# The order of TensorE's work within a slot: projections, transpositions, side work, scores and values

## The reference

```
for i in range(6):
    # 16 heads of 64; window of 32 tokens: each query sees its own and the previous 32
    q, k, v = split(shift_tokens(x) @ Wqkv[i])
    q, k = rotary(l2norm(q) * qs), rotary(l2norm(k) * ks)
    x = softmax(8 * q k^T, masked to the window) v @ Wo[i] + x
    xn = layernorm(shift_tokens(x)) * g + b
    a, gate = split(xn @ W1[i] + b1)            # 341 features each
    x = a * gelu(gate) @ W2[i] + b2 + x
out = xn0 + linear_branch * silu(x)
```

## Time and profile before

| | |
|---|---|
| median of three executions | 1900.61 us (1897.97 to 1902.92) |
| the profiled execution | 1898.34 us |
| its span, first to last instruction | 1896.5 us |
| TensorE busy | 1663.9 us, 88% |
| VectorE busy | 1436.9 us, 76% |
| ScalarE busy | 1345.7 us, 71% |
| GpSimd busy | 1298.5 us, 68% |
| mean granted TensorE clock | 0.971 |
| DMA | 66.13 MB, q1 at 11.5% of 16 engines |

### The profile page before, as it was taken

One profiled execution on the slowest core, in us unless ns is written; L12 is line 12 of the kernel. 1 busy time (PEld: TensorE's weight loads), 2 busy tenths in 40 slices (PEclk: granted clock), 3 DMA queues, 4 the chain that ended last, 5 costly groups with the idle time before them and its releaser, 6 DMA issues.

```text
span 1896.5 us, 68500 instructions
## 1 busy us (share of the span) xinstructions
PE 1663.9 (88%) x25968; PEld 1306.9 (69%) x26160; DVE 1436.9 (76%) x3041; ACT 1345.7 (71%) x2656; POOL 1298.5 (68%) x1283
## 2 busy tenths in 40 slices
PE   7789899899899899889989989988998998899873
PEld 5667677677677677767777766777777776677651
DVE  4488778777777777877777777777777778777755
ACT  4267777777777777777777777777777777777753
POOL 5277777776777777777677777767777776766730
PEclk9799999999999999999999999999999999999985
DMA  4011111011011011100111110011110001000000
GB/s 161 11 36 34 30 29 36 29 39 45 28 33 33 28 40 39 37 29 28 33 39 36 37 32 29 28 44 41 32 33 28 29 29 42 29 24 25 24 18 20
DMA packets 41406, 66.13 MB, mean 35 GB/s; under 512 B 7072, under 2 KB 16032, under 8 KB 41376
## 3 DMA queue, kind: packets, MB, share of 16 engines
q1 hardware_dynamic: 40224, 65.38, 11.5%
q10 hardware_dynamic: 1152, 0.34, 0.1%
HBM read 20.61 MB, written 1.05 MB: 11 GB/s over the span
## 4 chain that ended last, share of the span: by engine, by line
PE 51%; ACT 15%; DVE 14%; issue 12%; POOL 5%; DVEq 2%; ACTq 0%; DMA 0%; POOLq 0%
PE ps_f L490 11%; PE ps_qs L490 6%; PE ps_a L490 6%; PE ps_k L490 6%; PE ps_v L490 6%; POOL qk L426 5%; PE ps_qs L596 4%; ACT p_bd L838 4%; ACT squares L844 4%; PE ps_po L604 4%; PE ps_tk L596 4%; PE ps_po L490 3%; ACT L933 3%; PE ps_q L490 2%; DVE prob L1120 2%
## 5 line engine op out<-in xcount | busy, mean ns | idle before, releaser
L426 POOL TENSOR_TENSOR qk<-qk,rnorm 128x512 f32<-128x512 f32 x384 | 393.4, 1046 | 336.3 <-DVE rnorm L1110 336.3
L418 POOL TENSOR_TENSOR qk<-qk,qk_rot 128x512 f32<-128x512 f32 x384 | 488.3, 1282 | 95.0 <-DVE qk_rot L1077 85.6
L1083 DVE TENSOR_REDUCE ssq<-squares 128x8 f32<-128x512 f32 x384 | 249.8, 682 | 66.0 <-ACT squares L844 65.8
L838 ACT COPY p_bd<-ps_po 64x512 f32<-64x512 f32 x384 | 221.6, 577 | 60.1 <-PE ps_po L604 57.5
L490 PE MATMUL ps_qs<-k_t,q_t 64*32 64x64 f32 x12288 | 210.7, 218 | 50.1 <-ACT k_t L838 27.4
L433 POOL TENSOR_TENSOR prob<-prob,row_inv 128x512 f32<-128x512 f32 x192 | 200.9, 1046 | 64.0 <-DVE row_inv L1129 63.9
L1126 DVE TENSOR_REDUCE row_sum<-prob 128x8 f32<-128x512 f32 x192 | 131.8, 686 | 116.1 <-ACT prob L942 116.1
L490 PEld LDWEIGHTS ps_qs<-k_t,q_t 64*32 64x32 f32 x12288 | 179.7, 107 | 57.9 <-issue 57.9
L596 PE MATMUL ps_qs<-ident,qk 128*128 128x128 f32 x768 | 118.9, 278 | 113.0 <-POOL qk L426 112.5
L942 ACT ACTIVATE prob<-prob 128x512 f32<-128x512 f32 x192 | 121.2, 631 | 127.2 <-DVE prob L1120 124.1
L490 PEld LDWEIGHTS ps_po<-p_bd,v_back 128*64 128x64 f32 x3072 | 162.9, 137 | 48.6 <-issue 32.2
(11 more groups left out here) (161 smaller groups left out, 4007.5 us busy)
## 6 DMA issues: line engine op xcount, KB each, us to landing
v_back<-v_own SPq DMA_DIRECT2D x192, 192.0 KB, 2.4
w_raw<-in_wqkv SPq DMA_DIRECT2D x48, 192.0 KB, 2.4
v_back<-v_own SPq DMA_DIRECT2D x96, 64.0 KB, 2.1
wo_sb<-in_wo SPq DMA_DIRECT2D x12, 256.0 KB, 3.1
w_sb<-in_w SPq DMA_DIRECT2D x6, 341.0 KB, 3.4
w_sb<-in_w SPq DMA_DIRECT2D x6, 192.0 KB, 2.7
x_in<-in_x SPq DMA_DIRECT2D x4, 256.0 KB, 4.5
out<-s_out SPq DMA_DIRECT2D x8, 128.0 KB, 1.9
```

The lines of the kernel that those rows point to most:

```text
L418: nc.gpsimd.tensor_tensor(qk[:, s, i, :], qk[:, s, i, :], qk_rot[:, s, i, :], ALU.add).then_inc(added, 1)
L426: nc.gpsimd.tensor_tensor(heads(qk[:, s, i, :]), heads(qk[:, s, i, :]), rnorm[:, s, 8 * i:8 * i + 8].unsqueeze(2).to_broadcast([P, 8, HEAD ...
L838: return nc.scalar.copy(o, i)
L1083: V.tensor_reduce(ssq[:, s, 8 * i:8 * i + 8], heads(squares[:, s, OCTET * i:OCTET * i + OCTET]), AX, ALU.add).then_inc(ssq_done, 1)
```

## The change

In TensorE's `body`, the transposition of q moves from behind q's projection to behind v's projection, and that of k with it; the scores move behind the out projection and the FFN parts, directly ahead of the values. The order of a slot before and after:

| before | after |
|---|---|
| project q | project q |
| (slot 1: LN variance; slot 3: FFN part 1) | (slot 1: LN variance; slot 3: FFN part 1) |
| transpose q | (slot 2: LN spread) |
| (slot 2: LN spread) | project k |
| project k | (slot 0: LN mean) |
| (slot 0: LN mean) | project v |
| transpose k | transpose q |
| project v | transpose k |
| (slot 2: ff_down) | (slot 2: ff_down) |
| transpose p | transpose p |
| scores | (0: FFN part 2; 1, 3: out projection; 2: FFN part 0) |
| (0: FFN part 2; 1, 3: out projection; 2: FFN part 0) | scores |
| values | values |

```diff
@@ -737,21 +737,20 @@
                             ln_variance(n - 2)
                         if i == 0 and j == 3 and live_batch(n - 2):
                             ff_up(n - 2, 1)
-                        if live(u - 1):
-                            turn_qk(u - 1, i, (j - 1) % 2)
                         if i == 0 and j == 2 and live_batch(n - 2):
                             ln_spread(n, n - 2)
                     if isinstance(n, int) and u == 0:
                         bias_fold()
                     if live(u):
                         project(n, j, 2, ps_v, v_copied, v_done)
+                    if live(u - 1):
+                        turn_qk(u - 1, 0, (j - 1) % 2)
+                        turn_qk(u - 1, 1, (j - 1) % 2)
                     if j == 2 and live_batch(n - 3):
                         ff_down(n - 3)
                     if live(u - 2):
                         turn_p(u - 2, j % 2)
 
-                    if live(u - 1):
-                        scores(u - 1, (j - 1) % UNITS, (j - 1) % 2)
                     if j == 1 and live_batch(n - 1):
                         out_projection(n - 1, 0)
                     if j == 0 and live_batch(n - 3):
@@ -760,6 +759,8 @@
                         ff_up(n - 2, 0)
                     if j == 3 and live_batch(n - 1):
                         out_projection(n - 1, 1)
+                    if live(u - 1):
+                        scores(u - 1, (j - 1) % UNITS, (j - 1) % 2)
                     if live(u - 2):
                         values(u - 2, n if j >= 2 else n - 1, (j - 2) % UNITS, j % 2)
 
```

## The result

The changed kernel takes 1987.39 us (median of four, 1986.69 to 1995.89) against 1899.36 us before (four executions, in the same comparison): a ratio of 1.0471, 95% interval 1.0438 to 1.0503. The forecast was 1994 us, range 1938 to 2040, slower with 0.92. The profiled execution has a span of 1986.3 us.

The account below looks back on a forecast made before the run. The kernel was taken as bound by its batch period of 36.5 us, paced by the norms. Four links summed to 38.57, 2.07 more; over 45 batches 93 us, giving 1994 us, range 1938 to 2040.

Parts of the forecast that it names:

- link 0 to 1: Slot 0's norm to slot 1's: set by ScalarE, with TensorE in time; stays at 9.36 us.
- Link 1 to 2: Slot 1's norm to slot 2's: FFN part waits for after_ff, scores queue behind it; 10.97 us against 9.26.
- Rival A: Faster, TensorE the only bound, if after_ff ends before TensorE has transposed p in slot 2; 1791 us, chance 0.06.
- rival B: Slower by about half: link 1 to 2 grows less, slot 3 absorbs the out projection; 1932 us, chance 0.15.
- Link 2 to 3: Slot 2's norm to slot 3's: out projection now ahead of the scores, plus a wait for p; 8.70 us against 7.71.
- Link 3 to 0: Slot 3's norm to the next slot 0's: out projection leaves the link, v's projection waits; 9.54 us against 10.17.
- keep_v ends later ... a wait of 0.9: In link 3 to 0, v's projection waits 0.9 us for ScalarE's keep_v, until norm + 2.3.
- in time by half a microsecond: In link 0 to 1, TensorE's path through slot 1's scores to the norm takes 8.83 us, within 9.36.
- Move (b): Transposition of p right behind that of k, no projection between; p ready about 3.3 us after a norm.
- Rival D: TensorE's clock falls in slot 2 of each batch, at least 5 us more a batch; above 2200 us, chance 0.03.
- gaps of this size have not cost the clock: Read from slot 1, where the granted clock is 1.00 with a TensorE gap of 1.43 us.
- Rival C: Slower by half as much again: norm 1 missed too, every new wait costs a restart; 2045 us, chance 0.12.

Follow-up runs that it names:

- e1: The changed kernel with only slot 2's FFN part 0 put back behind the scores; 1927.1 us, ratio 1.0124 to the kernel before.
- e7: The changed kernel with VectorE doing after_ff ahead of slot 2's two sums of squares instead of behind the clamp; 1940.2 us, ratio 1.0219 to the kernel before.
- E6: The changed kernel with ScalarE's copy of v ahead of the exponential; 1993.42 us, ratio 1.0486 to the kernel before.
- E8: The changed kernel with a square in place of gelu and no preload, so without both table loads; 1981.33 us, ratio 1.0435 to the kernel before.
- E2: The changed kernel with out projections and FFN parts all behind the scores again, projections and transpositions as changed; 1906.64 us, ratio 1.0025 to the kernel before.
- e5: E2 with v's projection moved back between the transpositions of k and p; 1867.0 us, ratio 0.9828 to the kernel before.
- e4: The kernel before with only the out projections and FFN parts moved ahead of the scores; 2054.13 us, ratio 1.0794 to the kernel before.

## Why the prediction was right

**What was right.** The sign, the size (1994 for 1987) and the place. Per batch the forecast has 38.57 us and the trace 38.44. From the first norm of slot 3 to the last (137.11 to 1832.23 us before, 141.91 to 1922.21 after) the kernel takes 85.2 us longer, the head 4.8, and the drain the same; the span grew by 89.8.

That the batch came out within 0.13 us is in part luck. The links were off by -0.12, -0.30 and +0.28 us, which nearly cancel, and link 0 to 1 was right for only one of its two reasons.

**Link 1 to 2**, the main term: 10.97 forecast, 10.85 measured. After_ff ends 6.52 us behind norm 1 (forecast 6.58), the FFN part starts at 932.89, the scores are issued by 935.19 and the norm comes 1.86 later. That after_ff gates the FFN part, and with it the scores, is shown from both sides: e1 takes the scores out of the queue behind it (8.28), e7 makes after_ff earlier without touching TensorE (9.80). Rival A, in which after_ff would have been in time, and rival B, in which the link hardly grows, are out.

**Link 2 to 3**: 8.70 forecast, 8.40 measured. The step from the last issue of the scores to the norm was taken as 1.72 from slot 3 before. There find_max had still to wait for the clamp. Now the scores are last, find_max starts at once (944.25, the scores being issued by 943.09 + 1.02 = 944.11), and the step is 1.34. The rest of the link is as forecast: the scores of slot 2 are issued by 935.19 (934.17 + 1.02), the transposition of p starts 5.13 us later (forecast 5.15), and from there to the last issue of slot 3's scores it is 3.79 (3.68). The same step of 1.72 stands in link 3 to 0 as well.

**Link 3 to 0**: 9.54 forecast, 9.82 measured. The step "keep_v ends later ... a wait of 0.9" gave a right start for v's projection (norm 3 + 2.3; measured 909.49, + 2.47), but the wait is only 0.45 us and not 0.9, since TensorE is ready for it at norm 3 + 2.0 (907.02 to 908.44 + 0.60) and not + 1.35; and it is not the one cause. E6 removed it and gained 0.1: VectorE's rotations, behind the same exponential, set the squares just as late. The forecast followed one of two chains of nearly the same length.

**Link 0 to 1**: 9.36 both, but not for the reason given alone. The step "in time by half a microsecond" left out what TensorE waits for between the transposition of p and the out projection: var_ready, that is L1145 behind both rotations. E8 shows that TensorE's chain takes 9.32 by itself, and e6 that a delay on it shows at once. For the same reason the wait of 0.6 us that was forecast ahead of the spread in slot 2 is not there: TensorE gets to it at about the time of the norm (926.18, by the pitch of 0.23, and 926.20).

**Move (b)** was costed at a wait of 0.2 us in slot 3. There is none in the row at 940.32, but the transposition starts 0.55 us behind the one ahead, where it is 0.44 without a wait: 0.1 us. E2 against e5 shows its price where the side work does not cover the copy of k_t: 40 us.

**The clock** stayed up: mean granted 0.978 against 0.971 before, and 1.00 from 100 to 1915 us, though TensorE waits 1.44 us ahead of the FFN part in each batch. Rival D did not come about in the change. But the sentence "gaps of this size have not cost the clock" was read from one slot and does not hold: the same trace has seven batches with 3.4 us at 0.50 behind that very gap, and e4 has such a stretch in two batches of three. The page's slices are some 50 us wide and hide a stretch of 3.4. So the reason for putting D at 0.03 was weak. Its price was too high for such a fall, which costs 0.56 us of a batch before and 1.23 in e4, not 5. Why the gap of 1.44 us in slot 2 never costs the clock and that of 1.43 in slot 1 sometimes does, no run here shows. Rival D had beside it the Trainium skill's section "HAM oscillation" (TensorE: Matmul & The Clock Gate); the changed kernel shows no such falling back, while e4 shows it in most batches.

**The signs** that were named: q's wait is gone, the period is 38.4, and after_ff is the releaser, all as said. The wait for it is 1.44 us, just short of the 1.5 named, and v's is 0.76 in slot 1 but 0.45 in slot 0, where 0.7 or more was named for both. TensorE's idle time was put at 5.4 us a batch and is 4.28, because its busy time did not stay as it was.

**Rival C** needed norm 1 to be missed. By e8 it was nearer than its 0.12 said: the room was 0.04 us and not 0.5.

What stays open: in which batches the clock falls, and why. The step by which e6 is slower is 0.27 us in link 0 to 1, and its interval against the changed kernel does not exclude zero. In e5, where the remaining 60 us before the scores come from in each slot was not tried apart.

## What to carry to other kernels

When a loop is paced by a chain that visits several engines, cost a new order by the links of that chain, from one visit to the next, and look at what the moved work covered in its old place: here the order that removed 110 us of waits at one point put 160 at others. A moved instruction brings its own semaphore waits along, and everything behind it in the engine's order then waits too; the four matmuls that carried a wait for VectorE were 60 of the 88 us lost. How a cover is shared out among gaps matters: all three projections ahead of the transpositions of q, k and p gave 1907 us (e2), two ahead and v's between k and p gave 1867 (e5), and one ahead of each transposition 1899 (the kernel before). And look at the granted clock of each stretch, not only at its mean: two batches with the same waits differed by 1.23 us.

## What the runs showed that was not expected

The pitch of the same four transpositions depends on what follows: 0.35 us with a projection behind them (932.93 to 933.28 in the earlier trace rows), 0.44 with another transposition behind (910.27 to 910.71 and 911.15 after). A projection behind another one takes 0.70 (907.74 to 908.44) where it took 0.78 among transpositions, so the sum over a slot hardly changes. And TensorE's busy time rose by 53 us, 1.2 us a batch, for the same instructions in a kernel in which it waits more: a higher busy time is not more work done. Part of it is how a wait is counted. A wait starts only at the end of the matmul ahead: in slot 1 of the changed kernel that one starts at 916.58 and takes 0.40, and v's projection starts at 917.73 with a wait of 0.76. Without a wait the next one would start 0.23 behind, so 0.17 us more count as busy. Seven waits stand in a batch after and four before; how much of the 1.2 us that makes was not worked out.

The two chains of link 0 to 1 tie at 9.32 and 9.36 us. Removing 2.57 us from one of them gave 0.04 us a batch in the trace and nothing that the run times can tell.
